# The first quarter of x loaded from ScalarE's queue, and the sort's first sums moved behind the first product with the scaled B

## The reference, cut to what matters

```
h    = einsum('btc,erc->bter', x, As)               # 8 experts of rank 16
lora = einsum('bter,eor,be->bto', h, Bs, cond)      # weighted by cond, per batch
x    = x + (einsum('btc,oc->bto', x, W_base) + b_base) + lora * 2.0

rw   = softmax(cond);  w, sel = top_k(rw, 2);  w = w / w.sum()
x    = x + sum over the 2 chosen experts of w * mlp(x; that expert's gate, up, down)
         + mlp(x; shared gate, up, down)            # mlp = (gelu(x gate) * (x up)) down
```

## Time and profile before

| | us |
|---|---|
| median of 3 runs | 130.94 |
| lowest and highest | 130.9, 131.74 |
| the profiled execution | 130.7 |
| its span, first to last instruction | 129.0 |
| TensorE busy | 124.4 |
| VectorE, ScalarE, GpSimd busy | 90.4, 72.3, 61.4 |

### The profile page before, as it was taken

How to read it: one execution, slowest core, us unless ns; L and a number is a source line. 1 busy time by engine, 2 the same in 40 slices (tenths; PEclk the granted TensorE clock), 3 DMA queues, 4 the chain that set the end, 5 groups by cost and what they waited for, 6 DMA issues and landing times.

```text
span 129.0 us, 3154 instructions
## 1 busy us (share of the span) xinstructions
PE 124.4 (96%) x869; PEld 113.3 (88%) x869; DVE 90.4 (70%) x177; ACT 72.3 (56%) x136; POOL 61.4 (48%) x111
## 2 busy tenths in 40 slices
PE   6999999999999999999999999999999999999991
PEld 6657887878887889999999999999999999999990
DVE  2767988769979999543478767767777677766641
ACT  2484667976956777113566476557665756611110
POOL 5649464553796977552253643553365413610000
PEclk9999999999999999999999999999999999999999
DMA  3998888899000057589555586558799950023921
GB/s 55 271 332 298 292 239 275 231 295 283 21 3 0 0 194 286 175 323 422 239 224 231 196 333 262 208 201 307 264 323 315 381 180 0 3 73 97 287 64 53
DMA packets 14524, 26.56 MB, mean 206 GB/s; under 512 B 2224, under 2 KB 7600, under 8 KB 12976
## 3 DMA queue, kind: packets, MB, share of 16 engines
q1 hardware_dynamic: 14192, 26.35, 59.8%
q10 hardware_dynamic: 320, 0.07, 0.3%
HBM read 12.52 MB, written 1.31 MB: 107 GB/s over the span
## 4 chain that ended last, share of the span: by engine, by line
PE 91%; DVE 3%; DMA 1%; issue 1%; POOL 1%; DVEq 0%; POOLq 0%
PE bank L1044 11%; PE bank L1080 9%; PE bank L1081 9%; PE bank L1082 9%; PE bank L1062 6%; PE bank L991 6%; PE bank L993 6%; PE bank L992 6%; PE bank L1102 5%; PE bank L1103 4%; PE bank L1104 4%; PE bank L1007 3%; PE bank L1008 3%; PE bank L1009 3%; PE bank L916 3%; PE bank L924 2%
## 5 line engine op out<-in xcount | busy, mean ns | idle before, releaser
L556 ACT ACTIVATE work<-bank 128x512 f32<-128x512 f32 x48 | 28.7, 598 | 39.2 <-PE bank L1082 17.5
L714 DVE TENSOR_TENSOR bank<-bank,work 128x512 f32<-128x512 f32 x40 | 27.9, 699 | 18.3 <-PE bank L1082 13.1
L731 DVE TENSOR_TENSOR hT_lo<-bank,hT_hi 128x512 fp32r<-128x512 f32 x40 | 27.3, 682 | 1.0 <-issue 0.5
L1080 PE MATMUL bank<-xp,wst 128*128 128x256 f32 x96 | 27.3, 284 | 0.0
L1081 PE MATMUL bank<-xp,wst 128*128 128x256 f32 x96 | 27.2, 283 | 0.0
L1082 PE MATMUL bank<-xp,wst 128*128 128x256 f32 x96 | 27.2, 283 | 0.0
L483 POOL TENSOR_TENSOR wstd<-wexd,wstd 128x512 fp32r<-128x512 f32 x12 | 15.5, 1294 | 24.3 <-ACT wstd L598 24.3
L565 ACT CAST hT_hi<-bank 128x512 fp32r<-128x512 f32 x40 | 23.3, 583 | 1.6 <-DVE bank L714 1.6
L1081 PEld LDWEIGHTS bank<-xp,wst 128*128 128x128 f32 x96 | 18.4, 192 | 0.0
L1080 PEld LDWEIGHTS bank<-xp,wst 128*128 128x128 f32 x96 | 18.4, 192 | 0.0
L1082 PEld LDWEIGHTS bank<-xp,wst 128*128 128x128 f32 x96 | 18.4, 192 | 0.0
(11 more groups left out here) (153 smaller groups left out, 211.9 us busy)
## 6 DMA issues: line engine op xcount, KB each, us to landing
wst<-wex SPq DMA_DIRECT2D x12, 1024.0 KB, 4.7
raw_ex<-n_L_cond_skill_gate_dram SPq DMA_DIRECT2D x8, 256.0 KB, 3.1
raw_ex<-in_L_cond_skill_up_dram SPq DMA_DIRECT2D x8, 256.0 KB, 3.8
sst<-n_L_cond_skill_gate_dram SPq DMA_DIRECT2D x8, 256.0 KB, 3.7
sst<-in_L_cond_skill_up_dram SPq DMA_DIRECT2D x8, 256.0 KB, 4.2
xn<-in_x_dram SPq DMA_DIRECT2D x4, 256.0 KB, 4.3
out_dram<-xT SPq DMA_DIRECT2D x4, 256.0 KB, 2.7
sst<-_L_cond_shared_gate_dram SPq DMA_DIRECT2D x1, 256.0 KB, 4.6
```

What stands on the lines that cost most here:

```text
L556: act.activation(gelu_sb[q], gate_ps[q][:, :], ACT.Gelu_apprx_tanh).then_inc(gelu_done, 1)
L714: dve.tensor_tensor(up_ps[u][:, :], up_ps[u][:, :], gelu_sb[q], ALU.mult).then_inc(h_done, 1)
L731: dve.tensor_tensor(hT_lo[:, q, :], up_ps[u][:, :], f32(hT_hi[:, q, :]), ALU.subtract).then_inc(lo_done, 1)
L1080: pe.matmul(of_c, w_hi, x_hi, start=True, stop=False)
```

## The change

The load of the first group of x moves from the second place of SyncE's queue to the first place of ScalarE's, ahead of cond. On TensorE, the two matmuls of `sort_counts` move from ahead of `x_transposes(0)` to behind `delta_w(0)`. Nothing is added or left out.

```
         @block.sync
             sp.dma_start(b_nat[:, :, :], Bs.rearrange("e o r -> o e r")).then_inc(ld_b, 16)
-            sp.dma_start(xn[:, 0:GB, :], x[0:GB].rearrange("b s h -> s b h")).then_inc(ld_x[0], 16)
             sp.dma_start(w_nat[:, :], W_base).then_inc(ld_w, 16)
...
         @block.scalar
         def _(act):
+            act.dma_start(xn[:, 0:GB, :], x[0:GB].rearrange("b s h -> s b h")).then_inc(ld_x[0], 16)
             act.dma_start(cond_sb[:, :], cond).then_inc(ld_cond, 16)
...
-            sort_counts()
             x_transposes(0)
             pe.wait_ge(ld_w, 16)
             pe.transpose(bank[6][:, 0:H], w_nat[:, :], ident[:, :]).then_inc(setup_ps, 1)
             pe.wait_ge(ld_a, 16)
             delta_w(0)
+            sort_counts()
             pe.wait_ge(setup_sb, 3)
             x_transposes(1)
```

## The result

The median of five runs is 132.58 us (132.41 to 133.12) against 130.9 (130.76 to 131.74): ratio 1.0114, 95% interval 1.0077 to 1.015. The forecast was 131.0 within 130.4 to 131.7, so the time lies above the range, and the change makes the kernel 1.1% slower. The profiled execution took 133.12 us and its span 131.4, some 0.5 us above the median of its kernel. Ratios here leave out executions far above the fastest of their kernel, so they can differ a little from a quotient of medians.

A forecast was written before the change was run, and what follows sets the result against it. TensorE was taken to bound the kernel, with the shared expert's first gate matmul at 15.80 us. The larger of TensorE's -0.04 to +0.2 and VectorE's 0 to +0.25, taken as +0.1, moved median 130.94 to 131.0; range 130.4 to 131.7.

The forecast's parts named there:

- the landing of cond and Bs: Start of the load queues: Bs may come at 4.1 us instead of 3.37, cond at 4.15 instead of 2.60.
- the last of the two: The later of the Bs and x loads, sharing the engines, lands 3.3 us after 0.87, at 4.2 us.
- The second rival: Loads at the start: cond or Bs lands at 4.6 to 5.0 us, giving 131.4 to 131.8 us; chance 0.17.
- The second term: the clock: TensorE's first product takes 1.71 us at the low level, ending at 8.1, or 7.95 if the clock rises near 7.8.
- the third rival: TensorE's early idle time puts off the clock's rise from 7.8 to 10.8 us, giving 132.5 us; chance 0.07.
- From cond's landing to the first product: Start of TensorE's stream: cond lands at 4.15 us and the first product starts at 6.4.
- The counts: TensorE, behind the first product: they cost 0.19 us at the low level, some 0.1 at the high, without waiting.
- As: The 64 KB load two places behind x on ScalarE's queue is there by 5.0 us, ahead of its use.
- ScalarE's copy 1: ScalarE's x copy moves from 8.42 to about 10.4 us, ends at 11.0, covered by 0.5 us.
- The step on VectorE's line 702: Line 702, now blocked by GpSimd's line 374, ends at 13.40 us against 13.33; VectorE's line 0 to 0.25 later.
- the lock: VectorE and GpSimd share a port pair exclusively, the loser blocking; without it line 702 would run 12.0 to 12.7 us.

## Why the prediction was wrong

**The step that failed: the landing of cond and Bs.** I put "the last of the two" at 4.2 us and cond with it, by adding 0.8 us of Bs's pieces and 0.79 of x's, with 4.8 as the far end. Measured were 4.9 for Bs, 5.1 for x and 5.57 for cond (5.26 in another execution). The direction and the mechanism, cond behind x's bytes, were right; the term was mis-sized by 1.4 us. The sum took x's bytes at 332 GB/s from 2.57 us on. The core moved 99 GB/s from 2.5 to 3.0 and 281 to 310 from there to 5.5, so the two loads took longer than the sum of their works: 0.8 us longer for x, which landed at 4.3 once Bs was read in long rows. And cond came another 0.5 behind x. The second rival ("the loads are slower", 131.4 to 131.8) is this case, and it had reckoned with at most 5.0. By its own rule, the whole excess over 4.15, the measured landing gives some 132.4.

The rule of the Trainium skill named ahead of the result, in "DMA: Bandwidth & Descriptors", section "Queues, rings and completion order", that DMA engines take turns between queues and keep ring order within one, agrees with the runs in which something stood ahead of cond: it came at 4.02, 4.42 and 5.57 us behind 64, 128 and 256 KB, each time after the x ahead of it. That Bs took 4.0 us beside x instead of 2.5 fits the turns; with x issued 0.5 us later Bs took 2.5 again, so that run shows none. The rule was in the prediction and its size was not.

**The second term: the clock.** I let it rise at 7.8 us as before, or left the first product wholly at the low level. It rose at about 10.9 in the profiled execution and at about 12 in the repeated one, so the second transposes and part of the second product ran at half speed: 0.62 us in the first, and 1.37 in the second (1.04 and 1.71 for 0.52 and 0.86). That is the third rival, which I gave 0.07 and priced as if cond were on time. Its 132.5 lies beside the measured 132.58, and its 10.8 beside 10.9, by luck: it reckoned 1.5 us for the clock and nothing more for the loads, where the clock took 0.62 and the landing the rest. The two came together, since the late cond is what makes TensorE idle; they were not independent chances.

**What held, and what didn't come.** From cond's landing to the first product it was 2.11 us, against 2.25 reckoned (4.15 to 6.4). The counts cost 0.22 us in the stream, against 0.1 to 0.19, and didn't wait for the sort; their move as such is within the noise. As was there in time. ScalarE's copy 1 came 3.4 us later than before and was done at 12.42, well ahead of the second first-layer group at 13.94. The step on VectorE's line 702, "one stall in the place of the other", did not come about: it had assumed TensorE on time. The kept traces do bear on the lock named beside it. In the kernel with cond at the head of SyncE's queue TensorE was nearly on time, and line 702 ran into line 374 as foretold:

```profile
11.84 1.28 POOL L374 TENSOR_TENSOR wsh<-sst,wsh 128x512 fp32r<-128x512 f32 x1 [2.81 <-ACT wsh L540]
12.42 1.24 DVE L702 TENSOR_TENSOR wsh<-sst,wsh 128x512 fp32r<-128x512 f32 x1
```

It ended 0.54 us after GpSimd's instruction. In each of the thirteen traces in which the two overlap it ended 0.53 to 0.55 us after GpSimd's end, whatever its own start, and took 0.68 to 1.69 us; in the one without (the changed kernel repeated) it took 0.68.

**What stays open.** The clock's moment differs between executions of one kernel (the kernel before: 130.08 to 131.98 us over 27 runs), and no run fixed it. With ten warm-ups and TensorE busy from 1.2 us on, the high level came before 5.1 us in one profile and at about 7.2 in the other. Why an idle 0.3 us at 4.3 matters and 1 us before 3 us does not was not settled; the gain from filling the first is shown by the times, its way through the clock by one profile.

## What to carry to other kernels

A small load that the first instructions wait for belongs at the head of its queue, ahead of any large one: 0.5 KB behind 256 KB landed 3 us late. Moving the large load to another queue brought it later in the changed kernel and behind cond (5.1 and 5.0 us instead of 4.7); where it came earlier (4.1), another load paid for it. When an idle wait of TensorE at the start is taken away or added, work out TensorE's clock with it, as one case and not as a separate chance. And before a wait of TensorE is removed, try filling it with a matmul on zeros: that was worth more here than any order of the loads. Read TensorE's level from the durations of its matmuls, as the granted clock of the profile may not show it.

## What the runs showed of the hardware that was not expected

Two loads issued at the same moment on two queues, 64 KB in 64-byte pieces and 256 KB in 512-byte rows, moved 99 GB/s between 2.5 and 3 us; with the 64 KB in 512-byte rows it was 218. With the 256 KB issued 0.5 us later the 64 KB landed as in the kernel before (2.5 us after issue, against 4.0). And one matmul of 0.43 us at the low level, put into a gap of 0.31 us, brought the high level 1.8 us forward, from about 7.8 to 6.0 us, and the kernel's runs spread over 0.44 us (6 runs) instead of 1.9 (27 runs). The profile's granted clock read 1.00 where matmuls took twice their time. And a VectorE subtraction that met a GpSimd instruction ended 0.53 to 0.55 us after that one's end, in thirteen traces out of thirteen.
